# A transformer kernel on one core: 36 matmuls of each pair of steps made as two half-width ones, three waits dropped, seven small instructions put ahead

## The reference, cut to what matters

```python
for i in range(6):
    # shift half of the channels by one token, then attention in windows of 32,
    # each window seeing itself and the one before; 16 heads of 64
    q, k, v = split(shift(x) @ Wqkv[i], 3)             # 128 -> 3 x 1024
    q, k = rotary(l2norm(q) * qs), rotary(l2norm(k) * ks)
    x = softmax(mask(8 * q @ k.T)) @ v @ Wo[i] + x     # 1024 -> 128
    # shift, layernorm, gated feed-forward
    a, gate = split(layernorm(shift(x)) @ W1[i] + b1[i], 2)   # 128 -> 2 x 341
    x = (a * gelu(gate)) @ W2[i] + b2[i] + x
```

## Time and profile before

| | before |
|---|---|
| runs | 3230.7, 3246.5, 3247.95 us; median 3246.5 |
| the profiled execution | 3239.37 us, its span on the engines 3237.6 us |
| granted TensorE clock, mean of the span | 0.989 |
| TensorE matmuls busy | 96% of the span, x52802 |
| TensorE weight loads busy | 84%, x52802 |
| VectorE, ScalarE, GpSimd busy | 86%, 79%, 82% |
| chain that ended last | TensorE 88%, ScalarE 2%, "issue" 2%, GpSimd 1% |

### The profile page before, as it was taken

One profiled execution on the slowest core, in us unless ns is written; L12 is line 12 of the kernel. 1 busy time (PEld: TensorE's weight loads), 2 busy tenths in 40 slices (PEclk: granted clock), 3 DMA queues, 4 the chain that ended last, 5 costly groups with the idle time before them and its releaser, 6 DMA issues.

```text
span 3237.6 us, 123133 instructions
## 1 busy us (share of the span) xinstructions
PE 3121.0 (96%) x52802; PEld 2720.9 (84%) x52802; DVE 2769.2 (86%) x3716; ACT 2546.3 (79%) x3699; POOL 2647.6 (82%) x2646
## 2 busy tenths in 40 slices
PE   7988999999999999999999999999999999999997
PEld 4657888888888888888888888888888888888886
DVE  7978888888888888888888888888888888888884
ACT  5766788787878888787878877887878788878876
POOL 6758888887888888888888888887888888888873
PEclk9989999999999999999999999999999999999999
DMA  2001111111111111111111111111111111111111
GB/s 66 15 24 38 48 36 45 43 35 42 46 43 42 44 37 43 37 51 43 41 35 41 42 48 41 41 41 40 39 47 46 43 35 41 44 41 40 40 41 48
DMA packets 62044, 134.01 MB, mean 41 GB/s; under 512 B 11584, under 2 KB 35264, under 8 KB 61504
## 3 DMA queue, kind: packets, MB, share of 16 engines
q1 hardware_dynamic: 61504, 126.14, 13.5%
HBM read 21.27 MB, written 4.19 MB: 8 GB/s over the span
## 4 chain that ended last, share of the span: by engine, by line
PE 88%; ACT 2%; issue 2%; POOL 1%; DVE 0%; POOLq 0%; DVEq 0%
PE pair L215 71%; PE pair L218 17%; ACT qT L901 0%; ACT PT L882 0%; ACT X L920 0%; ACT X L906 0%; ACT sq L879 0%; ACT sq L891 0%; ACT VA L914 0%; ACT Sx L886 0%; POOL qk L1145 0%; POOL qk L1164 0%; DVE ss L1024 0%; DVE pair L1051 0%; DVE ts L1020 0%
## 5 line engine op out<-in xcount | busy, mean ns | idle before, releaser
L1164 POOL TENSOR_TENSOR qk<-qk,ts 128x1024 f32<-128x1024 f32 x384 | 910.5, 2383 | 70.5 <-DVE ts L1020 61.4
L1145 POOL TENSOR_TENSOR qk<-qk,rn 128x1024 f32<-128x1024 f32 x384 | 724.0, 1907 | 15.1
L1016 DVE TENSOR_TENSOR qk<-pair,tab 128x1024 f32<-128x1024 f32 x384 | 468.3, 1220 | 266.3 <-ACT sq L879 258.0
L879 ACT ACTIVATE sq<-pair 128x1024 f32<-128x1024 f32 x191 | 196.0, 1026 | 442.1 <-PE pair L215 441.9
L215 PE MATMUL pair<-wq_h,xs_h 128*128 128x512 f32 x1154 | 513.9, 445 | 2.5 <-issue 1.5
L1179 POOL TENSOR_TENSOR Sx<-Sx,rden 128x1024 f32<-128x1024 f32 x192 | 365.3, 1903 | 170.1 <-DVE rden L1096 170.1
L1020 DVE TENSOR_TENSOR ts<-pair,tab 128x1024 f32<-128x1024 f32 x384 | 466.4, 1215 | 0.0
L1024 DVE TENSOR_REDUCE ss<-sq 128x16 f32<-128x1024 f32 x384 | 464.3, 1209 | 0.0
L215 PE MATMUL pair<-wq_h,xs_l 128*128 128x512 f32 x1152 | 463.3, 402 | 0.1
L215 PE MATMUL pair<-wq_l,xs_h 128*128 128x512 f32 x1152 | 462.1, 401 | 0.6 <-issue 0.5
L218 PEld LDWEIGHTS pair<-small,qk 128*128 128x128 f32 x3072 | 350.2, 143 | 84.2 <-issue 53.0
(11 more groups left out here) (127 smaller groups left out, 6675.4 us busy)
## 6 DMA issues: line engine op xcount, KB each, us to landing
VB<-VA SPq DMA_DIRECT2D x192, 384.0 KB, 3.5
VB<-VA SPq DMA_DIRECT2D x96, 128.0 KB, 3.4
wq_raw<-wqkv SPq DMA_DIRECT2D x18, 512.0 KB, 5.1
xf<-xT SPq DMA_DIRECT2D x96, 64.0 KB, 1.9
xf<-xT SPq DMA_DIRECT2D x96, 63.8 KB, 2.0
wo_sb<-wo SPq DMA_DIRECT2D x6, 512.0 KB, 3.4
X<-x_in SPq DMA_DIRECT2D x4, 512.0 KB, 6.5
x_kept<-X SPq DMA_DIRECT2D x4, 512.0 KB, 2.7
```

Source lines behind the costliest of these rows:

```text
L879: A_.activation(sq[:, 0, :], one[:, :], ACT.Square).then_inc(S["squared"], 1)
L1016: V_.tensor_tensor(h3(qk[:, now, kind, :], DH), h3(source[:, :], DH), rep(factors[:, 2 * kind, b, :], HEADS, DH), ALU.mult)
L1145: G_.tensor_tensor(x, x, bc(rn[:, then, kind * HEADS:(kind + 1) * HEADS], HEADS, DH), ALU.mult).then_inc(S["scaled"], 1)
L1164: G_.tensor_tensor(qk[:, now, kind, :], qk[:, now, kind, :], ts[:, kind, :], ALU.add).then_inc(S["added"], 1)
```

## The change

It does three things. `project` makes the last `halved` of a projection's six matmuls as two matmuls of 256 columns each (all six in even steps and in q and k of odd ones, the last three in v of odd steps: 33 of 36 in a pair; a few less at the first step of a layer and late in the last layer). The last three of the 32 score matmuls of even steps are made as two of 32 columns. Two waits of TensorE that an earlier wait of the same step covers are left out: ahead of the transposes `f_xn` (odd steps), and ahead of the output projection (every step). Seven `apart` instructions stand ahead of TensorE's first wait.

```diff
+        AHEAD = 7
+        HALVED = {0: (6, 6, 6), 1: (6, 6, 3)}
+        SPLIT_SCORES = 3
+        def halved(pl, k):
+            t, n = pl.t, HALVED[pl.t % BLOCKS][k]
+            if k == 2 and t == NBLOCKS:
+                n -= 1 + pl.turn % 2
+            if k == 2 and pl.last and pl.seq(13) is not None:
+                n -= 2 + t // BLOCKS % 2
+            return n
-        def project(layer, pair, high, low, first):
+        def project(layer, halved, pair, high, low, first):
             w_high, w_low = wq_high[layer % 2], wq_low[layer % 2]
+            n = 0
             for u in range(2):
-                cols = slice(first + u * UNIT, first + (u + 1) * UNIT)
-                out = pair[:, u * UNIT:(u + 1) * UNIT]
-                mm(out, high, w_high[:, cols], True, False)
-                mm(out, low, w_high[:, cols], False, False)
-                last = mm(out, high, w_low[:, cols], False, True)
+                for x, w in ((high, w_high), (low, w_high), (high, w_low)):
+                    width = UNIT // 2 if n >= 6 - halved else UNIT
+                    for at in range(0, UNIT, width):
+                        last = mm(pair[:, u * UNIT + at:u * UNIT + at + width], x,
+                                  w[:, first + u * UNIT + at:first + u * UNIT + at + width],
+                                  n % 3 == 0 and at == 0, n % 3 == 2, skip_group_check=True)
+                    n += 1
             return last
...
-            project(0, pair, xs_h[:, 0, 0:P], xs_l[:, 0, 0:P], k * INNER).then_inc(S[name + "_done"], 1)
+            project(0, 0, pair, xs_h[:, 0, 0:P], xs_l[:, 0, 0:P], k * INNER).then_inc(S[name + "_done"], 1)
...
-                project(layer, one, high, low, 0).then_inc(S["q_done"], 1)
+                project(layer, halved(pl, 0), one, high, low, 0).then_inc(S["q_done"], 1)
...
-                if pl.has(0):
+                if pl.has(0) and pl.seq(11) is None:
                     e.wait_ge(S["rotated"], blocks(pl, "rotated", 0, 2))
-                elif q:
+                if not pl.has(0) and q:
                     e.wait_ge(S["x_kept"], seqs(pl, "x_kept", q - 1, 1))
...
-                            last = mm(PB[w * KEYS:(w + 1) * KEYS, to:to + KEYS], qT[:, a, 2 * pair + w, :],
-                                      kT[:, a, key0:key0 + KEYS], False, True, skip_group_check=True)
+                            width = WIN if b == 0 and 4 * a + 2 * pair + w >= 4 * PAIRS - SPLIT_SCORES else KEYS
+                            for at in range(0, KEYS, width):
+                                last = mm(PB[w * KEYS:(w + 1) * KEYS, to + at:to + at + width], qT[:, a, 2 * pair + w, :],
+                                          kT[:, a, key0 + at:key0 + at + width], False, True, skip_group_check=True)
...
-                if pl.has(1):
-                    e.wait_ge(S["qkT_kept"], blocks(pl, "qkT_kept", 1, 2))
-                else:
+                if not pl.has(1):
                     e.wait_ge(S["pT_kept"], blocks(pl, "pT_kept", 3, 1))
...
         def _(pe):
+            for _ in range(AHEAD):
+                apart(pe)
             pe.wait_ge(S["c_loaded"], 16)
```

More of the change, by code:

```diff
@@ L708, in step_pe @@
                     e.wait_ge(S["wq_low_k"], layers(pl, 2, t // NBLOCKS, 2))
-                project(layer, other, high, low, INNER).then_inc(S["k_done"], 1)
+                project(layer, halved(pl, 1), other, high, low, INNER).then_inc(S["k_done"], 1)
             if pl.has(1):
@@ L742, in step_pe @@
                     e.wait_ge(S["wq_low_v"], layers(pl, 2, t // NBLOCKS, 2))
-                project(layer, one, high, low, 2 * INNER).then_inc(S["v_done"], 1)
+                project(layer, halved(pl, 2), one, high, low, 2 * INNER).then_inc(S["v_done"], 1)
             if pl.has(1):
```

## The result

| | before | after |
|---|---|---|
| median of 4 runs each | 3246.93 us | 3294.22 us (3291.7 to 3297.08) |
| ratio after to before, 95% interval | | 1.0162 (1.0137 to 1.0187) |
| the profiled execution, its span | 3239.37, 3237.6 us | 3291.7, 3289.9 us |
| granted TensorE clock, mean of the span | 0.989 | 0.985 |

The account below looks back on a forecast made before the run. TensorE's own stream was taken to bound the kernel. From 3239.4 us, 64.2 of stalls were taken off and 33 added (0.345 a pair, 96 pairs), giving 3208 us, range 3180 to 3240.

Parts of the forecast that it names:

- What bounds the kernel: TensorE's own stream, busy 96% of the span, with 64.2 us lost to 41 instruction-fetch stalls at packet edges.
- Place of the crossings: Packet edges would fall 13, 61, 141 or 189 instructions into AV, all seen without a stall: 64.2 us gone.
- Rival 1: Packets beginning in the q projection come late, so AV stalls at 189: +65 us, 3273 us; chance 0.13.
- Halved projections and split scores: On TensorE, projection matmuls and score passes made in two add 0.165 and 0.19 us a pair of steps.
- The crossing at 13: Every second even step, an edge 13 instructions into the v projection costs 0.2 us, 47 times; bounds 0 and 0.67.
- rival 2: The v projection stalls in full, 0.67 us each in every second even step: +22 us, 3230 us; chance 0.09.
- The waits and the seven: TensorE's three removed waits count for nothing; the seven added instructions run while it waits for its first load.
- Rival 3: Packet edges cost nothing by themselves; the stalls belong to something else in AV and stay: 3270 us; chance 0.04.

## Why the prediction was wrong

**What bounds the kernel** held: TensorE's stream, and the stalls at edges of packets. That an AV stage of 2.00 us runs through a packet faster than a late one comes was right too: with 3.5 us of work in its place, no AV stalled.

**Place of the crossings** is the step that failed, and in it one sentence: "Each of 13, 61, 141 and 189 occurs in the trace of before without a stall", from which "I take the 64.2 us as gone". The count was right to the instruction (13, 61, 141, 189, one or two off in later layers). But the place does not decide alone: in the changed kernel 36 of 43 crossings at that place stalled and 7 passed, with twelve small instructions 15 and 28. In the kernel before the crossing wandered, and a passing 189 in an odd step came one step behind a stall at 222. In the changed kernel the places ahead of 189 are always 141, 61 and 13, where AV doesn't stall; a stall ahead of it stood only at the edge behind the crossing at 13, in 7 of the 43. I counted one row as an independent observation, and didn't look at what stood 512 instructions ahead of it. Against the forecast's sum this step is wrong by 77.2 us of the 83.7 between 3208 and the profiled 3291.7.

**Rival 1** had the place, the sign and nearly the price: it expected 38 of 43 crossings at 189 to stall and 3273 us; 37 of 45 did. The rest is a stall's price, 1.72 instead of 1.57 us, and the ends of the program. Its reason was wrong: with twelve instructions at the start, or with k whole, the packet still begins in the q projection and most crossings pass. Its 0.13 was too low, because all that spoke against it was the same row.

**Halved projections and split scores** were right: 0.355 us a pair by the sum, 0.31 in the pairs without a stall and 0.32 in the kernel with v ahead of AV, where no stall is near. **The crossing at 13** cost less than the 0.2 us taken (eight of 45, 0.28 each), and its sign is another than I gave it: where the v projection stalls, the dearer stall in AV is saved. The kernel with 16 instructions at the start shows rival 2 in full, 45 stalls and 3236 us for its 3230. **The waits and the seven** cost nothing that shows.

**Start and end** were not in the sum beyond the six pairs' share of the halves (2 us); they grew by 11.4.

**Rival 3** is out: all 45 stalls of the changed kernel stand at an edge. The rule that I set beside it, from the Trainium skill ("Runtime: NRT & Kernel Launch", section "Instruction fetch mechanics"), that a crossing is "mostly hidden", agrees with the traces for some 400 of 449 crossings; the other 45 cost 77 us in the changed kernel.

What stays open: why the packet before the late one is requested 7.4 to 8.1 us ahead of AV in one odd step and 10.5 to 11.1 in another, with the waits between the two requests at the same times ahead of AV, and why a stall of 0.2 us changes it. The runs show that the two go together, not how.

## What to carry to other kernels

Where instructions run faster than their packets arrive, aligning the stream to packet edges fixes one pattern for the whole run; before building on a place that was "seen clean", look at what preceded it each time it was seen. Rather than to count instructions, put slower work (here wide matmuls) ahead of or into the run of small ones, and move waits that are already over away from its front. Ahead of the run, the first took the stall from 0.95 to 0.4 us (with work on the other engines that the new order needed); into it, it took all stalls away and cost about as much as they had. The second on top took the 0.4 to none; alone it left 0.65 us.

## What the runs showed of the hardware that I had not expected

- A late packet's request follows the sequencer's last wait instruction ahead of the run by 1.06 to 1.17 us (medians in six kernels), though that wait was over by then every time (its instruction took 51 ns): the last wait passed at 0.80, 1.05, 1.42 and 2.40 us ahead of AV gave requests at +0.32, +0.08, -0.30 and -1.19 us. This is no rule for all requests: the packet before the late one in the changed kernel came 1.6 to 2.3 us behind the wait instruction before it.
- Stalls in AV of the changed kernel come in steps: most are 1.00, 1.27 or 1.55 us long.
- Every stretch of the lower clock in the steady parts followed a stall of 0.83 us or more; none followed the 45 stalls of up to 0.9 us in the kernel with 16 instructions at the start, and 31 of the 45 in the changed kernel, up to 1.29 us long, had none behind them.
- A float32 pass of 64 columns on 128x128 weights takes no less than one of 128: 22 passes of the output projection, 12 of them of 64 columns, took 2.47 us, 16 whole ones 1.81.
